# Which adapter halves run in float32r parts: block 0 in float32 as a whole, blocks 1 and 2 with both halves split

## The reference, cut to what matters

```python
h = x * (scale[:, None, :] * rsqrt(ms + EPS)); u = h @ up_w.T
val, gate = split(u, 2); h = val * gelu(gate)
x = act_quant(h) @ weight_quant(down_w).T + x
down = relu(einsum('bld,bnd->bln', x, Wd_b) + bd)      # the adapter
up = einsum('bln,bdn->bld', down, Wu_b) + bu
return x + up
```

## Time and profile before

| | |
|---|---|
| median of 3 runs | 839.96 us (838.9 to 840.93) |
| the profiled execution | 840.44 us, its span 838.7 us |
| TensorE busy | 821.2 us, 98% |
| VectorE busy | 664.3 us, 79% |
| ScalarE busy | 399.8 us, 48% |
| GpSimd busy | 121.3 us, 14% |
| DMA | 186.65 MB, mean 223 GB/s |
| idle of TensorE ended by `seed_c` (c_ps, line 1915) | 3.6 us in 6 places |

### The profile page before, as it was taken

The page is one execution under the profiler, slowest core; times in us unless marked ns, Lnnn a source line. Parts: engine busy times, 40 slices in busy tenths (PEclk is TensorE's granted clock), DMA queues, the critical chain, the costliest instruction groups (busy, mean ns, idle before and its releaser), DMA issues.

```text
span 838.7 us, 11856 instructions
## 1 busy us (share of the span) xinstructions
PE 821.2 (98%) x3914; PEld 359.4 (43%) x3914; DVE 664.3 (79%) x968; ACT 399.8 (48%) x653; POOL 121.3 (14%) x91
## 2 busy tenths in 40 slices
PE   5999999999999999999999999999999999999998
PEld 4334444444344334444444444444444444444443
DVE  5998787889878889767787678988986586675986
ACT  5778887776454532227445543326433333324000
POOL 0363332302001153300101011100200000001000
PEclk9999999999999999999999999999999999999999
DMA  9879989666899862377798865337247435435232
GB/s 343 338 257 347 343 289 297 233 217 226 303 347 366 330 218 95 136 271 272 280 326 303 304 223 191 116 95 255 72 137 239 138 95 189 138 95 176 101 125 76
DMA packets 64860, 186.65 MB, mean 223 GB/s; under 512 B 7072, under 2 KB 8352, under 8 KB 64416
## 3 DMA queue, kind: packets, MB, share of 16 engines
q1 hardware_dynamic: 64512, 185.63, 63.5%
q10 hardware_dynamic: 288, 0.26, 0.1%
HBM read 154.41 MB, written 30.41 MB: 220 GB/s over the span
## 4 chain that ended last, share of the span: by engine, by line
PE 85%; DVE 5%; issue 3%; ACT 1%; DVEq 0%; ACTq 0%
PE b_ps L1351 9%; PE b_ps L1355 9%; PE b_ps L1353 9%; PE aux_ps L1406 6%; PE a_ps L1351 6%; PE aux_ps L1464 6%; PE a_ps L1355 6%; PE a_ps L1353 6%; PE c_ps L1351 3%; PE aux_ps L1542 3%; PE e_ps L1351 3%; PE e_ps L1355 3%; PE e_ps L1353 3%; PE c_ps L1353 3%; PE c_ps L1355 3%
## 5 line engine op out<-in xcount | busy, mean ns | idle before, releaser
L1954 DVE SCALAR_TENSOR_TENSOR h_ring<-v_sb,unscale,gelu 128x512 f32<-128x512 f32 x63 | 55.5, 881 | 58.0 <-ACT gelu L1092 31.9
L1351 PE MATMUL b_ps<-t_mov,u_l 128*128 128x512 f16 x252 | 95.5, 379 | 3.8 <-DVE c_ps L1915 3.6
L1355 PE MATMUL b_ps<-t_mov,u_l 128*128 128x512 f16 x252 | 95.5, 379 | 0.0
L1353 PE MATMUL b_ps<-t_mov,u_l 128*128 128x512 f16 x252 | 95.5, 379 | 0.0
L1978 DVE TENSOR_TENSOR hmax<-gelu,hmax 128x512 f32<-128x512 f32 x120 | 88.6, 740 | 7.8 <-ACT gelu L1098 2.9
L1068 ACT ACTIVATE b_ps<-a_ps 128x512 f32<-128x512 f32 x63 | 36.7, 582 | 94.1 <-PE a_ps L1355 93.9
L1102 ACT ACTIVATE gelu<-h_ring 128x512 f32<-128x512 f32 x64 | 40.3, 629 | 67.6 <-DVE h_ring L1954 67.6
L2013 DVE TENSOR_TENSOR h_ring<-h_ring,qscale 128x1024 f16<-128x1024 f32 x48 | 64.7, 1387 | 0.0
L1084 ACT ACTIVATE gelu<-a_ps,unscale 128x512 f32<-128x512 f32 x64 | 43.7, 682 | 43.3 <-DVE hmax L1978 41.1
L916 POOL PARTITION_ALL_REDUCE yscale<-hmax x8 | 17.9, 2266 | 321.0 <-DVE hmax L1978 320.3
L1098 ACT ACTIVATE gelu<-h_ring 128x512 f32<-128x512 f32 x64 | 40.2, 628 | 45.6 <-DVE h_ring L1964 45.3
(11 more groups left out here) (264 smaller groups left out, 1701.4 us busy)
## 6 DMA issues: line engine op xcount, KB each, us to landing
w_ring<-in_Wdu SPq DMA_DIRECT2D x64, 512.0 KB, 6.0
w_ring<-in_Wdd SPq DMA_DIRECT2D x56, 512.0 KB, 7.2
u_l<-ul_dram SPq DMA_DIRECT2D x48, 512.0 KB, 4.7
u_e<-ue_dram SPq DMA_DIRECT2D x48, 384.0 KB, 3.2
h_ring<-in_up_w SPq DMA_DIRECT2D x16, 512.0 KB, 6.4
x_sb<-in_x SPq DMA_DIRECT2D x8, 1024.0 KB, 7.9
res<-in_down_w SPq DMA_DIRECT2D x16, 512.0 KB, 7.1
ul_dram<-u_l SPq DMA_DIRECT2D x15, 512.0 KB, 5.6
```

The lines of the kernel that those rows point to most:

```text
L1351: pe.matmul(ps[:, :], weight(n, p, 0, k), hi, start=fresh and k == 0, stop=False, skip_group_check=True)
L1353: pe.matmul(ps[:, :], weight(n, p, 0, k), lo, start=False, stop=False, skip_group_check=True)
L1355: mm = pe.matmul(ps[:, :], weight(n, p, 1, k), hi, start=False, stop=k == 1, skip_group_check=True)
L1954: dve.scalar_tensor_tensor(out=h_slot(n)[:, TB:TS], in0=val[:, :], scalar=unscale[:, s // 2, j:j + 1], in1=gelu2[:, :], op0=ALU.mult, op1= ...
```

## The change

- `SPLIT` is now the pair of blocks (1, 2). Block 0 runs both halves in float32: its relu goes straight to `stage`, its `mid_low` is gone.
- For blocks 1 and 2 the down half is split too: new `x_high` (ScalarE, two copies of 128x1024) and `x_low` (VectorE, two subtractions of 128x1024) make the parts of the input in `x_parts`, which shares the place of `x_sb`; `weight_high`, `down_weight_low` and `up_weight_low` split both weights, in quads 49 (ScalarE), 51 and 53 (VectorE).
- `x_high(1)` runs at the end of ScalarE's quad 50; `x_high(2)` in ScalarE's quad 53, its first half between `seed_b` and `keep_p5`, its second between `absolute1` and `gate1`. It waits for `load_ad(2)` and for the down half of block 1. `x_low` runs in quads 51, 53 (behind `val2`) and 54.
- Since `x_parts` takes the place of `x_sb`, the last two loads of `x` move from quads 50 and 53 to 56 and 57, behind the down half of block 2.
- In the last stage the quantising moves: none in quad 51, three chunks instead of two in quads 53 and 56.
- Two pairs of semaphores are merged, with the same waits as before.

```diff
--- before.py
+++ after.py
@@ -164,6 +164,7 @@
...
 QUANTISE = {3: 2, 4: 2, 5: 2, 6: 2, 7: 2, 8: 2, 9: 2, 10: 1}
+QUANTISE_LAST = {4: 2, 5: 3, 6: 2, 7: 2, 8: 3, 9: 2, 10: 1}
 Y_FIRST = 10
...
@@ -171,6 +172,7 @@
...
 NEXT_X = {2: 0, 5: 1}
+LAST_X = {56: 0, 57: 1}
...
@@ -193,9 +195,17 @@
...
 MID_AT = {49: 0, 52: 1, 55: 2}
-SPLIT = len(MID_AT)
+SPLIT = (1, 2)
+LAST_SPLIT = 2
+X_LOW = {51: ((1, 0), (1, 1)), 54: ((2, 1),)}
+X_LOW_LATE = {53: (2, 0)}
 UP_AT = {n + 1 + k // 2: (i, (k, k + 1)) for n, i in MID_AT.items() for k in (0, 2)}
+def part_at(i):
+    return (0, 2, 4)[i]
...
@@ -261,13 +271,14 @@
...
             mid_parts = first.enter_context(nc.sbuf_tensor("mid_parts", [P, 2, TB], F32R))
+            x_parts = first.enter_context(nc.sbuf_tensor("x_parts", [P, 2, KD, TB], F32R))
         res = sb("res", [P, 4, TB])
         stage = sb("stage", [P, 2, TB])
+        x_sb = sb("x_sb", [P, 2, KD, TB])
         u_e = sb("u_e", [P, 2, 2, 768], F16)
...
         h_ring = sb("h_ring", [P, SLOTS, TS])
-        x_sb = sb("x_sb", [P, 2, KD, TB])
         wq = sb("wq", [P, NP, D], F8)
...
@@ -531,7 +542,7 @@
...
                 "p5": (s_x1, 2 * KD * i + 6 + key[-1] + 1),
-                "mid": (s_part_lo, at + 2) if at < SPLIT else (s_relu, at + 1),
+                "mid": (s_part_lo, part_at(i)) if i in SPLIT else (s_relu, at + 1),
                 "up": (s_out, KD * at + key[-1] + 1),
...
@@ -733,7 +744,9 @@
...
-                if s:
+                if s == NSB:
+                    aux_ready(sp, "mid", LAST_SPLIT)
+                elif s:
                     sp.wait_ge(s_tlo, 7 * s + 1)
...
@@ -824,8 +837,10 @@
...
                     load_l(n + 1)
-                if j in NEXT_X:
+                if s + 1 < NSB and j in NEXT_X:
                     load_x(s + 1, NEXT_X[j])
+                if n in LAST_X:
+                    load_x(s + 1, LAST_X[n])
                 if s == 1 and Y_FIRST <= j < Y_FIRST + 4:
...
@@ -1161,23 +1176,36 @@
...
                 act.wait_ge(s_x_c22, 2 if at < 3 else 4)
-                if at >= SPLIT:
+                if i not in SPLIT:
                     act.activation(stage[:, at % 2, :], bank("mid", i)[:, :], ACT.Relu,
...
                 act.wait_ge(s_relu, at + 1)
-                if at:
-                    aux_ready(act, "up", ADAPTERS[at - 1], KD - 1)
+                aux_ready(act, "up", i - 1, KD - 1)
                 act.activation(mid_parts[:, 0, :], bank("mid", i)[:, :], ACT.Copy)\
...
-            def up_weight_high():
+            def weight_high():
                 act.wait_ge(s_l1w, 3)
...
                     act.wait_ge(s_res_put[h], 16 * 6)
+                    act.wait_ge(s_c22_put[h], 16)
+                act.activation(up_parts[:, 2, :], l1_wd[:, 0, :, :].rearrange("p k n -> p (k n)"),
+                               ACT.Copy).then_inc(s_part_hi, 1)
                 act.activation(up_parts[:, 0, :], l1_wu[:, 0, :], ACT.Copy).then_inc(s_part_hi, 1)
+            def x_high(i, halves=(0, 1)):
+                act.wait_ge(s_ad[i % 2], 16 * (i // 2 + 1))
+                if i == 1:
+                    act.wait_ge(s_tlo, split_count(NSB - 1, T4))
+                else:
+                    aux_ready(act, "mid", i - 1)
+                for half in halves:
+                    rows = slice(2 * half, 2 * half + 2)
+                    act.activation(x_parts[:, 0, rows, :], ad_slot(i)[:, rows, :], ACT.Copy)\
+                        .then_inc(s_x_hi, 1)
...
@@ -1220,6 +1248,8 @@
...
                     t_high(s + 1, B11)
+                if n == 53:
+                    x_high(2, (0,))
                 if j == 0:
...
@@ -1248,6 +1278,8 @@
...
                 absolute1(n - 1)
+                if n == 53:
+                    x_high(2, (1,))
                 if j == 0 or n == 1:
...
@@ -1265,8 +1297,10 @@
...
                     stage_group(g)
-                if n == NQ - NP - 2:
-                    up_weight_high()
+                if n == 49:
+                    weight_high()
+                if n == 50:
+                    x_high(1)
                 if n in MID_AT:
...
@@ -1536,6 +1570,18 @@
...
                     pe.wait_ge(s_ad[i % 2], 16 * (i // 2 + 1))
+                if i in SPLIT:
+                    pe.wait_ge(s_part_lo, 1)
+                    for k in range(KD):
+                        if k % 2 == 0:
+                            pe.wait_ge(s_x_lo, 2 * i - 1 + k // 2)
+                        hi, lo = (up_parts[:, 2 + n, P * k:P * k + P] for n in range(2))
+                        x_hi, x_lo = (x_parts[:, n, k, :] for n in range(2))
+                        pe.matmul(ps[:, :], hi, x_hi, start=(k == 0), stop=False)
+                        pe.matmul(ps[:, :], hi, x_lo, start=False, stop=False)
+                        mm = pe.matmul(ps[:, :], lo, x_hi, start=False, stop=(k == KD - 1))
+                    mm.then_inc(s_aux, 1)
+                    return
                 for k in ks:
...
@@ -1547,9 +1593,8 @@
...
                 at = ADAPTERS.index(i)
-                if at < SPLIT:
-                    pe.wait_ge(s_part_lo, 1)
-                    pe.wait_ge(s_part_lo, at + 2)
+                if i in SPLIT:
+                    pe.wait_ge(s_part_lo, 3 if i == 1 else 4)
                     cols = slice(P * k, P * k + P)
...
@@ -2113,14 +2158,28 @@
...
+            def down_weight_low():
+                dve.wait_ge(s_part_hi, 1)
+                dve.tensor_tensor(up_parts[:, 3, :],
+                                  l1_wd[:, 0, :, :].rearrange("p k n -> p (k n)"),
+                                  up_parts[:, 2, :].bitcast(F32), ALU.subtract)\
+                    .then_inc(s_part_lo, 1)
             def up_weight_low():
-                dve.wait_ge(s_part_hi, 1)
+                dve.wait_ge(s_part_hi, 2)
                 dve.tensor_tensor(up_parts[:, 1, :], l1_wu[:, 0, :],
...
+            def x_low(i, half):
+                rows = slice(2 * half, 2 * half + 2)
+                dve.wait_ge(s_x_hi, 2 * i - 1 + half)
+                dve.tensor_tensor(x_parts[:, 1, rows, :], ad_slot(i)[:, rows, :],
+                                  x_parts[:, 0, rows, :].bitcast(F32), ALU.subtract)\
+                    .then_inc(s_x_lo, 1)
             def mid_low(i):
-                dve.wait_ge(s_part_hi, ADAPTERS.index(i) + 2)
+                dve.wait_ge(s_part_hi, i + 2)
                 dve.tensor_tensor(mid_parts[:, 1, :], bank("mid", i)[:, :],
...
@@ -2231,7 +2290,7 @@
...
                         x_scaled(key[1])
-                    elif key[0] == "mid":
+                    elif key[0] == "mid" and key[1] in SPLIT:
                         mid_low(key[1])
...
@@ -2259,12 +2318,19 @@
...
                     scales(s, 0)
-                if s > 0 and j in QUANTISE:
-                    first = 1 + sum(v for q, v in QUANTISE.items() if q < j)
-                    quantise(s - 1, range(first, first + QUANTISE[j]))
+                chunks = QUANTISE_LAST if s == NSB - 1 else QUANTISE
+                if s > 0 and j in chunks:
+                    first = 1 + sum(v for q, v in chunks.items() if q < j)
+                    quantise(s - 1, range(first, first + chunks[j]))
                 if s > 1 and j == 10:
...
                     token_sums(s - 1, 3)
+                for i, half in X_LOW.get(n, ()):
+                    x_low(i, half)
+                if n == 51:
+                    down_weight_low()
+                if n == 53:
+                    up_weight_low()
                 if n in ASSEMBLE:
...
@@ -2301,8 +2367,8 @@
...
                 val2(n)
-                if n == NQ - NP - 1:
-                    up_weight_low()
+                if n in X_LOW_LATE:
+                    x_low(*X_LOW_LATE[n])
                 if n == 1:
...
                 if n == 3:
```

More of the change, by code:

```diff
@@ L457, in build @@
         s_first_lo = sem("s_first_lo")
-        s_sums_hi = sem("s_sums_hi")
-        s_sums_lo = sem("s_sums_lo")
         s_sums_put = sem("s_sums_put")
@@ L499, in build @@
         s_out = sem("s_out")
+        s_x_hi = sem("s_x_hi")
+        s_x_lo = sem("s_x_lo")
         s_part_hi = sem("s_part_hi")
@@ L574, in put_sums @@
             def put_sums():
-                sp.wait_ge(s_sums_lo, 2)
+                sp.wait_ge(s_first_lo, 3)
                 sp.dma_start(ue_dram[0].rearrange("p (a m) -> p a m", a=2)[:, :, 256:768],
@@ L643, in load_c11 @@
                 if d == 2:
-                    aux_ready(sp, "up", SPLIT - 1, KD - 1)
+                    aux_ready(sp, "up", LAST_SPLIT, KD - 1)
                 for h in range(2):
@@ L893, in weight_sums @@
                     if j == 6:
-                        pool.wait_ge(s_sums_lo, 2)
+                        pool.wait_ge(s_first_lo, 3)
                     pool.wait_ge(s_ulo, part_count(j - 2, 3))
@@ L1029, in sums_high @@
                 act.activation(s_split(pair)[:, 0, :], s_sum(0, 2 * pair, 2 * pair + 2), ACT.Copy,
-                               scale=um_mul[:, 0:1]).then_inc(s_sums_hi, 1)
```

(7 more changed lines are left out.)

## The result

The changed kernel takes **845.0 us** (median of six runs, 842.49 to 846.98) against 839.83 us before: a ratio of 1.0066, 95% interval 1.0053 to 1.0078. On another chip the ratio was 1.0064 (1.0046 to 1.0082). A ratio is estimated from the single runs of both kernels and isn't quite the quotient of the two medians (1.0062 here). It is slower, as forecast, and within 0.6 us of the forecast of 845.6. Times are of runs in the chip's usual state: one execution of e5 with 1238.08 us at a mean granted clock of 0.659 is left out.

A forecast was written before the change was run, and what follows sets the result against it. TensorE's queue, 98% busy, was taken to bound the kernel. Terms -0.68 - 0.48 + 5.43 = +4.27 us on a median of 839.96 gave 844.2; the lower clock's +1.4 made 845.6 us, range 842.6 to 847.6.

The forecast's parts named there:

- What bounds it: Quads 49 to 57: TensorE's queue, 98% busy, held through gate2 on ScalarE, multiply2 and seed_c on VectorE, then product 7.
- TensorE's own work: Block 0's up pairs to float32, +0.34 twice; down halves of blocks 1 and 2 to float32r, -0.68 twice: -0.68 us.
- The stall of quad 50: Without block 0's mid_low, seed_c comes 0.60 us earlier, so product 7's whole wait in quad 50 goes: -0.48 us.
- New work beside the path: Weight copies, input copies, low parts and later x loads on ScalarE, VectorE and the sync queue: cost taken as 0.
- The wait: Quad 53: ScalarE's x_high(2) waits for load_ad(2), landing at 644.41, delaying gate2, seed_c and product 7: a 5.43 us stall.
- What is late next: VectorE after the stall: seed_c of quad 54 is in time by 0.3 us, quad 56 has 0.5 us left.
- The clock: Behind quad 53's stall TensorE runs at the 1.2 GHz level for 2.8 us, half lost: +1.4 us, bounds 0 and 2.8.
- The sum: -0.68 - 0.48 + 5.43 = +4.27 us, giving 844.2; with 1.4 us for the lower clock, 845.6.
- Rival 1: Quad 53's stall occurs but TensorE keeps the full rate behind it: 844.2 us; chance 0.33.
- Rival 2: Block 2's load lands before it is missed: 838.8 us, or 840.5 with a 1.7 us stall; chance 0.10.
- Rival 3: Block 2's load takes 8.4 us instead of 5.8: +2.6, 846.8 at full rate, 848.2 with the lower; chance 0.08.
- Rival 4: The float32r down halves of blocks 1 and 2 cost as much as float32: +1.4 us; chance 0.02.

The follow-up runs named there:

- e5: The changed kernel with 20 unused float16 matmuls put ahead of product 7 of quad 53 in TensorE's queue: 844.02 us, ratio 1.0055 to the kernel before.
- e7: e1 with the down halves of blocks 1 and 2 in float32 again, without x_high and x_low: 839.07 us, ratio 0.9997 to the kernel before.
- e1: The changed kernel with block 0's store and block 2's load moved ahead of the u loads in the sync queue's quad 52: 837.37 us, ratio 0.9984.
- e6: e1 with the quantising back as before, two chunks in each of quads 51 to 57: 838.07 us, ratio 0.9985 to the kernel before.
- e8: The changed kernel again as it is, beside the others on the same chip: 844.46 us, ratio 1.0064 to the kernel before.
- e2: The changed kernel with block 2's input copies at the end of ScalarE's quad 53, its low parts in quads 54 and 55: 837.38 us, ratio 0.9982.
- e4: The changed kernel with block 0's store ahead of quad 52's u_l load, so store and load are issued earlier: 839.58 us, ratio 1.0008.
- e3: The kernel before plus only a ScalarE wait for block 2's load behind seed_b of quad 53: 843.99 us, ratio 1.0059.

## Why the prediction was right, step by step

- **What bounds it.** TensorE's queue, and in it the chain gate2, multiply2, seed_c, product 7. Right: every wait found in these quads, in every kernel here, ends with seed_c.
- **TensorE's own work, -0.68.** Right. A split down half takes from 630.68 + 0.22 to 633.89 - 0.22, 2.77 us (2.76 in the sum), in TensorE's timeline of the changed kernel:

```profile
630.68 0.38 PE L1389 MATMUL b_ps<-t_mov,u_l 128*128 128x512 f16 x1
...
633.89 0.38 PE L1387 MATMUL a_ps<-t_mov,u_e 128*128 128x512 f16 x1
```

- **The stall of quad 50, -0.48.** Right: TensorE has no idle entry between 590 and 640 us after the change, while the kernel before has the one of the earlier trace rows. e7 shows it with the float32 ups together.
- **New work beside the path, 0.** Right: without the wait (e1) the whole sum is -1.21 against -1.16, so nothing of the copies, low parts and later x loads reached the path. The cover of the moved quantising was thin, by e6: 0.6 us of it would have shown.
- **The wait, +5.43.** Right in place and mechanism, 0.75 too long: 4.68. Of this the store gives 0.47 (the load was issued 7.77 us after it, not 8.24), and 0.20 is from adding ScalarE's durations where it starts the next operation earlier (copy to keep_p5 0.97, not 1.05; keep_p5 to gate2 0.48, not 0.60). The load's 5.8 us, the steps of 0.78, 0.67 and 0.84 behind gate2 all came out within 0.02.
- **What is late next.** Right: seed_c of quads 54 and 56 held nobody. In the changed kernel TensorE's lower rate gave VectorE more room, but e5 is a hard test: there the full rate follows a stall, and seed_c of quad 54 is 0.69 us early (656.94 + 0.84 = 657.78, and product 7 starts at 658.47), where 0.3 was forecast.
- **The clock, +1.4.** Right that it falls, wrong in size: the lower level lasted from 646.13 to 651.60. The 13 starts in it take 5.47 us, and at the full rate 7 x 0.2156 + 1.38 = 2.89 (seven float16 starts, six float32r ones), so 2.58 us were lost. The step that failed is the length of the stretch, taken as 2.8 us from the kernel's start. There the 5.32 us of idling did not stand directly ahead of the dense matmuls: from 7.19 to 17.47 us small matmuls kept TensorE busy for 7.08 of 10.28 us. Behind the stall of quad 53 nothing of the kind had run. Whether that makes the difference is not shown. My upper bound of 2.8 held the 2.58; the 2.85 of e8 is just past it.
- **The sum.** -0.68 - 0.48 + 4.68 + 2.58 = +6.10, and +6.08 is measured from quad 49 on. The forecast had 5.67. Two errors of opposite sign, -0.75 and +1.2, leave 0.4; the medians moved by 5.2, because executions differ by a microsecond or two ahead of the changed part. The forecast's closeness of 0.6 us is partly luck. That nothing is missing from the sum, six profiles show: take the stall (in e5 the 5.36 us by which product 7 is late) and what the lower rate lost off the span from quad 49 on, and the changed kernel twice, e1, e2, e4 and e5 all leave 239.16 to 239.23 us.

The rule from the Trainium skill (TensorE: Matmul & The Clock Gate, "HAM oscillation — how this bites in real kernels"), that a burst after a wait for a DMA starts cold, agrees with this trace: a clock of 0.51 behind 4.68 us of idling. It did not come out so behind the shorter waits for the same load, 1.80 us in e4 and 3.18 in e3, whose traces show the full rate.

**Rivals.** Rival 1, the stall at the full rate, is what e3's profiled run did with 3.18 us, not the changed kernel with 4.68. Rival 2, the load in time, is e1, at the -1.2 us it was given; its variant with a short stall is e4 (1.80 us, 1.7 given). Rival 3, the slow load, didn't come: 5.5 to 6.0 us in the six kernels that issue it where its neighbours are the same or nearly so. In e1, e6 and e7, with other loads issued right behind it, it took 7.1 to 7.8. Rival 4 is excluded by the 2.77 us.

**A version that beats both.** e1 and e2 are faster than the kernel before: by 1.2 us from quad 49 on, ratios 0.9984 and 0.9982, both intervals below 1. The idea of the change is sound; its wait was in the wrong place.

## What to carry to other kernels

When a second engine becomes a reader of a loaded tile, look up when that tile lands in the old trace, not only when its old reader needed it: here the load landed at 644.2 before the change, 21 us before TensorE's down half at 665.63, and that was no slack for a copy two quads earlier. Put a wait on a transfer behind the latency-critical work in an engine's order, not between its steps. When TensorE bounds the kernel and its queue stalls for as long as here, 4.7 us, add the lower clock behind it to the price of the stall; behind 1.8 us there was nothing to add.

## What the runs showed of the hardware

- Stalls of TensorE after dense work: 1.80 us (e4) and 3.18 us (e3) were followed by the full rate in the profiled run, 4.68 us by 5.47 us at the 1.2 GHz level and 4.83 us (e8) by 5.95, so that a stall cost 1.55 and 1.59 times its length. All ten runs of the changed kernel have a mean clock of 0.995 to 0.998. At which length the clock falls, and whether it is a matter of luck, stays open.
- Filling the stall with 4.5 us of matmuls (0.88 us of idling left) kept the clock at 1.00.
- At the kernel's start the granted clock reads 1.00 while matmuls run 0.42 us apart; in the middle it reads 0.51 for the same pace. The column can't be trusted at the start.
- The same 1 MB store landed in 7.8 to 8.2 us where it was issued 0.4 us behind a 512 KB load, in 6.4 us where it was issued 0.9 us ahead of it (e4), and in 4.5 us with no load near it (e1, e6, e7).
